# Small arrays allocated behind the large ones: one SBUF offset for all large tiles of a fused conditioned linear attention

## What is computed

```python
xn = _ln(x, ln_w, ln_b)
q = softmax((xn @ Wq + bq) by head, over the head's 64 features)
k = softmax((xn @ Wk + bk + (1.0 - src_mask) * -1000000.0) by head, over the tokens)
v = ((xn @ Wv + bv) * src_mask) by head
att = jnp.einsum('bnhd,bnhl->bhdl', k, v)
y = jnp.einsum('bnhd,bhdl->bnhl', q, att).reshape(b, t, d)
scale, shift = split(silu(emb) @ W_emb + b_emb)
hh = _ln(y, ln2_w, ln2_b) * (1.0 + scale) + shift
hh = silu(hh) @ W_out + b_out
return x + hh
```

## Time and profile before

| | us |
|---|---|
| median of 3 runs | 483.63 |
| lowest, highest | 482.94, 485.74 |
| the profiled execution | 484.99 |
| its span, first to last instruction | 483.2 |

### The profile page before, as it was taken

The page is one execution under the profiler, slowest core; times in us unless marked ns, Lnnn a source line. Parts: engine busy times, 40 slices in busy tenths (PEclk is TensorE's granted clock), DMA queues, the critical chain, the costliest instruction groups (busy, mean ns, idle before and its releaser), DMA issues.

```text
span 483.2 us, 7324 instructions
## 1 busy us (share of the span) xinstructions
PE 464.2 (96%) x2478; PEld 371.8 (77%) x2478; DVE 363.3 (75%) x879; ACT 263.1 (54%) x485; POOL 132.8 (27%) x148
## 2 busy tenths in 40 slices
PE   4999999998899999999999999999899999989997
PEld 2677876885688878888888888888588868878875
DVE  6979976775878956979678658675988628888963
ACT  5333332321788523347555655655988814777882
POOL 0013311120200000104223233332410133676675
PEclk9999999999999999999999999999999999999999
DMA  8945310112133200110213212121322000233354
GB/s 284 356 168 207 121 43 7 46 46 102 43 121 98 88 26 19 45 43 1 82 28 132 84 49 87 45 87 45 131 85 69 0 1 23 89 131 124 123 172 149
DMA packets 23093, 43.50 MB, mean 90 GB/s; under 512 B 1992, under 2 KB 2064, under 8 KB 23056
## 3 DMA queue, kind: packets, MB, share of 16 engines
q1 hardware_dynamic: 21968, 40.93, 24.7%
q10 hardware_dynamic: 1088, 2.10, 1.2%
HBM read 34.64 MB, written 8.39 MB: 89 GB/s over the span
## 4 chain that ended last, share of the span: by engine, by line
PE 83%; DVE 8%; ACT 3%; issue 3%; POOL 1%; DMA 1%; POOLq 0%; DVEq 0%; ACTq 0%
PE ps L1154 21%; PE ps L1156 21%; PE ps L1155 21%; PE ps L1159 8%; PE ps L1330 5%; ACT ps L407 2%; PE ps L1255 1%; PE ps L1308 1%; DVE th L916 1%; PE ps L1227 1%; PE ps L1208 1%; DMA x_in<-in_x_dram 1%; DVE yst_raw L661 1%; DVE kf L798 1%; DVE qs L762 1%
## 5 line engine op out<-in xcount | busy, mean ns | idle before, releaser
L577 POOL TENSOR_TENSOR qs<-qs,qmax 128x512 f32<-128x512 f32 x32 | 35.9, 1122 | 192.8 <-DVE qmax L767 192.8
L1154 PE MATMUL ps<-ek_hi,zm_hi 128*128 128x512 f32 x128 | 51.5, 402 | 3.7 <-DVE ek_lo L803 2.1
L1154 PE MATMUL ps<-wk_hi,zT_hi 128*128 128x512 f32 x124 | 51.5, 415 | 1.7 <-DVE kf L748 1.7
L1154 PE MATMUL ps<-wq_hi,zT_hi 128*128 128x512 f32 x128 | 52.3, 409 | 0.3 <-DVE qs L762 0.3
L1156 PE MATMUL ps<-wq_hi,zT_lo 128*128 128x512 f32 x128 | 50.6, 395 | 0.0
L1155 PE MATMUL ps<-wq_lo,zT_hi 128*128 128x512 f32 x128 | 50.5, 395 | 0.0
L306 ACT ACTIVATE zT_hi<-ps 128x512 fp32r<-128x512 f32 x32 | 19.1, 596 | 57.6 <-PE ps L1159 57.6
L1156 PE MATMUL ps<-ek_hi,zm_lo 128*128 128x512 f32 x128 | 50.4, 394 | 0.0
L1155 PE MATMUL ps<-ek_lo,zm_hi 128*128 128x512 f32 x128 | 50.3, 393 | 0.0
L1156 PE MATMUL ps<-wk_hi,zT_lo 128*128 128x512 f32 x124 | 49.0, 395 | 0.0
L1155 PE MATMUL ps<-wk_lo,zT_hi 128*128 128x512 f32 x124 | 49.0, 395 | 0.0
(11 more groups left out here) (230 smaller groups left out, 1163.2 us busy)
## 6 DMA issues: line engine op xcount, KB each, us to landing
x_in<-in_x_dram SPq DMA_DIRECT2D x32, 512.0 KB, 3.5
res<-in_x_dram SPq DMA_DIRECT2D x32, 256.0 KB, 2.8
out_dram<-res SPq DMA_DIRECT2D x32, 256.0 KB, 2.0
y<-in_L_cond_Wk_dram ACTq DMA_DIRECT2D x2, 512.0 KB, 5.3
kf<-in_L_cond_Wq_dram ACTq DMA_DIRECT2D x1, 1024.0 KB, 8.1
eq<-in_L_cond_W_out_dram SPq DMA_DIRECT2D x1, 1024.0 KB, 8.5
wv_mod<-in_L_cond_Wv_dram SPq DMA_DIRECT2D x1, 1024.0 KB, 10.7
eq<-in_L_cond_W_emb_dram SPq DMA_DIRECT2D x4, 256.0 KB, 4.4
```

Source lines behind the costliest of these rows:

```text
L577: pool.tensor_tensor(q_heads, q_heads, qmax[:].unsqueeze(2).broadcast_to([P, H, DH]), ALU.subtract).then_inc(s["q_shift"], 1)
L1154: pe.matmul(o, a[0], bb[0], start=start, stop=False)
```

## The change

Ten small arrays are allocated behind the large ones. No instruction is added, removed, resized or moved on any engine, and no wait changes; all rows of the programs are the same but for the line numbers (one line more ahead of the functions). Only SBUF addresses differ.

```diff
         ident = sb("ident", [P, P])
         part = sb("part", [P, P])
+        x_in = sb("x_in", [P, XR, D])
+        zT_hi, zT_lo = sb("zT_hi", [P, 2, NB, P], F32R), sb("zT_lo", [P, 2, NB, P], F32R)
+        kf = sb("kf", [P, T, D])
+        eq = sb("eq", [P, T, D])
+        qs = sb("qs", [P, D])
+        km = sb("km", [P, D])
+        zm_hi, zm_lo = sb("zm_hi", [P, HI, D], F32R), sb("zm_lo", [P, LO, D], F32R)
+        ek_hi, ek_lo = sb("ek_hi", [P, HI, D], F32R), sb("ek_lo", [P, LO, D], F32R)
+        y = sb("y", [P, YR, D])
+        eqT = sb("eqT", [P, 2, NB, P])
+        u, th = sb("u", [P, D]), sb("th", [P, D])
+        res = sb("res", [P, RR, D])
+        att = sb("att", [P, NB, YW])
         ones = sb("ones", [P, 32])
         pick = sb("pick", [P, B])
         cols = sb("cols", [P, ROWS])
...
         ab = sb("ab", [P, B, 2, NB])
-        x_in = sb("x_in", [P, XR, D])
-        zT_hi, zT_lo = sb("zT_hi", [P, 2, NB, P], F32R), sb("zT_lo", [P, 2, NB, P], F32R)
-        kf = sb("kf", [P, T, D])
-        eq = sb("eq", [P, T, D])
-        qs = sb("qs", [P, D])
         qmax = sb("qmax", [P, H])
-        km = sb("km", [P, D])
         kcol = sb("kcol", [P, NB])
-        zm_hi, zm_lo = sb("zm_hi", [P, HI, D], F32R), sb("zm_lo", [P, LO, D], F32R)
-        ek_hi, ek_lo = sb("ek_hi", [P, HI, D], F32R), sb("ek_lo", [P, LO, D], F32R)
-        y = sb("y", [P, YR, D])
-        eqT = sb("eqT", [P, 2, NB, P])
-        u, th = sb("u", [P, D]), sb("th", [P, D])
-        res = sb("res", [P, RR, D])
-        att = sb("att", [P, NB, YW])
         rz = sb("rz", [P, NB])
```

## The result

| | before, us | after, us |
|---|---|---|
| median of 6 runs each | 483.52 | 480.55 |
| lowest, highest | 482.94, 485.74 | 479.98, 482.56 |
| profiled execution, its span | 484.99, 483.2 | 481.38, 479.6 |

A forecast was written before the change was run, and what follows sets the result against it. PE bounds the kernel, busy for 96% of the span, so the distance between 512-column matmuls sets the time. Gains of 2.4 and 1.2 us make 3.6: 483.6 - 3.6 = 480.0 us, range 477.8 to 483.5.

The forecast's parts named there:

- The mechanism: K, Q and O matmuls: operands at equal remainders by 512 run faster, Q behind K 2.72 to 2.74 us, from 2.81.
- The control in the old trace: Batch 1's outputs: moving `wo_*`, stationary `wk_*` (same remainder) 2.84 us a block against `zT_*` 2.88, same neighbours.
- the blocks behind a short product, 61 x 0.04: K, Q and O blocks right behind a short product: 61 on the path gain 0.04 us each, 2.4 us.
- The other term, 15 x 0.08: Q, K and O blocks following another block without a break: 15 gain 0.08 us each, 1.2 us.
- The prediction's lower bound of 2.1 us: Lowest total gain given beside 3.6 us, with 0.03 us for a block behind a short product and 0.06 otherwise.
- Both DVE stretches: At 335 to 349 and 414 to 428 us DVE's work is on the chain; gains made before them should be kept.
- No change: Rival for the whole kernel: operands' relative place does not set the pace, time stays 483.6 us; chance 0.22.
- equality by a larger unit, 2048: Rival reading: weights at 128 and `zT_*` at 1152 by 2048 would still be unequal; given little chance.
- More than forecast: Rival: transposes' operands become equal too, all 1032 matmuls fall from 233 to 227.5 ns, 5.7 us, to 477.8; chance 0.06.
- Luck: Rival, DVE stretch: two GpSimd hold-ups (2.2 us) and a clock fall (1.7 us) may go; 477 us, chance 0.05.
- Slower: Rival: DVE instructions fall into other GpSimd ones, 1.1 us each, a second clock fall 1.7; 486 us, chance 0.05.
- The transfers: Only the first load of x is on the chain, 4.8 us at most; its new place changes 0.2 us either way.
- the 11 ns that the prediction left open: ACT's copy from `th`: 621 ns into `zm_hi`, 632 into `wk_hi`; could gain or lose some 0.2 us in the last stage.

The follow-up runs named there:

- the gaps of 128 and 256 bytes: Two runs: the changed kernel with 128 or 256 unused bytes between `part` and `x_in`, moving the loops' arrays against the weights; 483.78 and 480.36 us at full clock.
- the experiment on G: Changed kernel with 32 unused bytes ahead of `ek_hi` and `ek_lo` and 480 behind, making G an unequal pair; median 483.02 us, ratio to before 0.9973.

## Why the prediction was right, and where it was off

**The mechanism** held in each place it was read from. The forecast had Q behind K at 2.72 to 2.74 us (2.72), K with Q at 5.57 (5.55), a K block in the loop at 2.84 (2.85), G unchanged at 2.72, `zT_*` outputs like `wk_*` ones (2.85, 2.86). The control in the old trace, outputs with two places of the stationary operand and the same neighbours, was what made the difference between stages trustworthy; the experiment on G showed the same from the other side. The unit, which the old trace could not give, is 256 bytes. By it the old pairs of K and Q (128 and 416) differ by 32 and those of the outputs in `zm_*` and `ek_*` (128 and 480) by 96. What no run separates is which pair it is. Weight loads run beside the matmuls (PEld is busy for 77% of the span and PE for 96%), and within one product all stationary parts share a remainder and all moving parts too, so it may be a matmul's own two operands or its moving operand and the next weight load.

**The size** was 3.6 us forecast, some 3.1 read from the timelines, 2.9 from the second bias product on between the gaps of 128 and 256 bytes, and 3.0 in the medians. At full clock the changed kernel is 2.9 us below the kernel before on one chip (480.48 and 483.38) and 3.4 on another (480.05 and 483.45). The term that was too large is that of the blocks behind a short product, 61 x 0.04. The 0.04 was the difference to six `wk_*` blocks with a mean of 2.842 us. In the changed kernel K has 2.846, Q 2.843, `zT_*` 2.844, outputs in `zm_*` 2.853 and in `ek_*` 2.852, and the `wk_*` blocks themselves 2.851. Against the old 2.88 that is 0.035: 2.1 us instead of 2.4. The other term, 15 x 0.08, came nearly as forecast: 0.077 for each Q, 0.06 for the K behind an output. The one output behind a Q went the other way, 2.849 before and 2.896 after, but the same block takes 2.858 and 2.828 in the other two profiles of the changed kernel. With it the term is 1.0 us. The prediction's lower bound of 2.1 us does not follow from the 0.03 it names, which with 0.06 gives 2.7; 0.02 for a block would give 2.1. Nor did all unequal blocks keep to 224 to 236 ns before they settled: one in `zT_*` starts with 240 and 238.

**Which path it came by** was right too. From the second bias product to batch 0's G the difference went from +0.43 to -0.94, 1.37 us, and two blocks ahead of that product add 0.12; the forecast had "some 1.5". The loop gave 1.54 for a forecast 1.8, and the outputs little, since there the chain goes over DVE and ACT. Both DVE stretches kept the gain that came before them.

**No change** is refuted: the relative place of the two operands costs 2.80 against 2.72 us for twelve matmuls. It is the case to which the prediction had put two rules of the Trainium skill. The Trainium skill's page "TensorE: Matmul & The Clock Gate", section "Step-by-step: what each phase is for", has two independent read ports; that the place of one operand relative to the other cannot matter was the prediction's inference from it, and the measurement is against it. The 16-byte lines of the Trainium skill's page "SBUF — State Buffer", section "Specifications (TRN2)", do not explain a unit of 256 bytes. The measurements decide. That equality by a larger unit, 2048, might be needed did not come true: 256 is enough.

**More than forecast** did not come. With the transposes' operands equal too, the first distances of a block still scatter: after a transpose, 12 starts of K in the loop take 2.85 us and not 2.72, as the `wk_*` blocks did before.

**Luck** came in part, and differently: both held-up DVE instructions stayed, and only the clock did not fall in the profiled run. The forecast priced that at 1.7 us, half of the 3.4. The timelines show 1.41, because the stretch begins 0.3 us before PE has work, and 0.95 once the waits for `ek_lo` behind it are taken off. The runs of the kernel before differ by 2.0 between their groups of clock, which is more than either; what else goes with the fall was not tried. That the profiled execution came to 481.38 us where the forecast had 481.4 is luck as well: its 3.6 us hold 0.95 from the clock and miss 0.5 lost at the start.

**Slower** had its point at several new collisions; the two known ones stayed in place and were as long.

**The transfers** were bounded at 0.2 us for a change of layout. No layout effect was found, but from one profile of the changed kernel to another the start moved by up to 1.7 us, so the bound was too narrow for comparing two single profiles, and the same holds for the clock.

## What to carry to other kernels

Where TensorE bounds a kernel, give the stationary and the moving operands of its long matmuls the same remainder by 256 bytes; a small array between large ones breaks this silently, and a gap mends it as well as a new order does. Read such an effect from the distance between starts, in runs of matmuls long enough to settle, and look for two places of one operand within one stage as a control. The gain here was 2.8% of the pace in long runs, 1.2% in blocks of twelve between short products, and 0.6% of the time. All of it is measured on one kind of matmul, 512 columns in the reduced type with a weight load for each; others were not tried.

## What the runs showed of the hardware that was not expected

Matmuls of 512 columns with a weight load for each went at 227 ns from start to start with operands equal by 256 bytes, and at 233 to 234 ns with differences of 32, 64 or 128 bytes. The pace is not reached at once: behind a transpose, a product y or an idle stretch the first distance is longer (0.31 to 0.34 us), the next five to nine mostly scatter in the equal pairs too, between 224 and 240 ns, and then they settle at 226 and 227. Why the relative place matters, and why 256 is the unit, no run here shows.

The other users of the arrays show nothing of it. DVE's `km<-km,kf` has a median of 692 ns before and after, though its inputs are at one remainder now; matmuls of a product y start 112 ns apart and transposes 109, before and after, with 1 ns of difference at most; and ACT's copy from `th` takes 620 ns into `zm_hi` and 632 into `wk_hi` after the change, where all are at one remainder, as it did before:

```profile
L307 ACT ACTIVATE zm_hi<-th x6: 618/620/630, 220.9 to 326.8; 128x512 fp32r<-128x512 f32 x6
...
L307 ACT ACTIVATE wk_hi<-th x5: 617/632/633, 377.8 to 467.9; 128x512 fp32r<-128x512 f32 x5
```

So the 11 ns that the prediction left open are not the offset's.
